# A selective-scan layer on one Trainium2 core: the convolution's taps and part of the sums over states change engine

## The reference

```python
x, z = split(layernorm(h) @ in_proj_w)            # 2048 channels each
xc = conv_b
for k in range(4):                                # depthwise causal convolution
    xc = xc + conv_w[:, k:k+1] * xp[:, :, k:k+Lq]
xc = silu(xc)
ssm_p = xc @ x_proj_w.T                           # 64 + 16 + 16 columns, each part rms-normalised
dt = softplus(dt_r @ dt_proj_w.T + dt_bias); A = -exp(A_log)
h_t = exp(dt*A) * h_{t-1} + dt * B_t * xc_t       # 16 states for each channel, t = 0..4095
ys = sum over the 16 states of h_t * C_t
y = (ys + D_param * xc) * silu(z)
x = x + y @ out_proj_w.T
x = x + layernorm(x) @ W_dequantised.T + bias
```

## Time and profile before

| | |
|---|---|
| median of 3 runs | 4657.14 us (4652.04 to 4660.07) |
| the profiled execution | 4652.27 us, span 4650.4 us |
| TensorE matmul, share of the span | 95% |
| TensorE weight load | 86% |
| VectorE | 90% |
| ScalarE | 76% |
| GpSimd | 87% |
| granted TensorE clock, mean | 0.98 |
| DMA, queue of SP, share of 16 engines | 39.6% |

### The profile page before, as it was taken

One profiled execution on the slowest core, in us unless ns is written; L12 is line 12 of the kernel. 1 busy time (PEld: TensorE's weight loads), 2 busy tenths in 40 slices (PEclk: granted clock), 3 DMA queues, 4 the chain that ended last, 5 costly groups with the idle time before them and its releaser, 6 DMA issues.

```text
span 4650.4 us, 80289 instructions
## 1 busy us (share of the span) xinstructions
PE 4425.4 (95%) x26656; PEld 4020.1 (86%) x26656; DVE 4164.3 (90%) x5745; ACT 3537.7 (76%) x8848; POOL 4034.5 (87%) x2942
## 2 busy tenths in 40 slices
PE   7788999999999999999999999999999999998879
PEld 6577889989898998989899898998989899897769
DVE  3899999999999999999999899999999999999871
ACT  3787787877878787787878878787887878777650
POOL 0898989989899998989899899999989999899870
PEclk9889999999999999999999999999999999999889
DMA  7324344353544435353444535335353443533232
GB/s 252 135 82 160 104 156 147 121 184 129 184 137 159 147 129 179 137 181 128 150 156 137 186 122 184 128 131 191 120 184 129 175 144 115 184 129 135 96 106 84
DMA packets 160286, 678.57 MB, mean 146 GB/s; under 512 B 21120, under 2 KB 30080, under 8 KB 110720
## 3 DMA queue, kind: packets, MB, share of 16 engines
q1 hardware_dynamic: 141440, 639.88, 39.6%
q10 hardware_dynamic: 18432, 33.56, 1.9%
HBM read 618.32 MB, written 55.05 MB: 145 GB/s over the span
## 4 chain that ended last, share of the span: by engine, by line
PE 65%; DVE 14%; POOL 8%; issue 7%; DMA 3%; ACT 2%; SPq 1%; POOLq 0%; DVEq 0%; ACTq 0%
PE gx L594 15%; PE ys L574 13%; PE g L767 12%; PE ys L614 12%; DVE hb L1378 9%; PE g L689 6%; POOL dbx L486 5%; DVE hc L1326 3%; POOL half L494 2%; PE ys L604 2%; PE ys L624 2%; PE hb L875 1%; DVE gx L1270 1%; DMA b_scratch<-ssmT 1%; DMA ybuf<-in_wf_scales 1%
## 5 line engine op out<-in xcount | busy, mean ns | idle before, releaser
L1378 DVE TENSOR_TENSOR_SCAN hb<-hb,dbx 128x512 f32<-128x512 f32 x2048 | 2496.7, 1219 | 110.8 <-ACT hb L1083 77.2
L486 POOL TENSOR_TENSOR dbx<-dtx,bb 128x1024 f32<-128x1024 f32 x1024 | 2421.2, 2364 | 68.9 <-DVE hb L1378 43.9
L1083 ACT ACTIVATE hb<-dt,a_neg 128x256 f32<-128x256 f32 x4096 | 1789.3, 468 | 66.3
L494 POOL TENSOR_TENSOR half<-hc 128x512 f32<-128x512 f32 x1024 | 1305.3, 1275 | 86.0 <-DVE hc L1326 85.1
L1326 DVE TENSOR_TENSOR hc<-hb,cb 128x512 f32<-128x512 f32 x2048 | 1376.2, 672 | 0.0
L574 PE MATMUL ys<-half,ident 128*128 128x256 f32 x4096 | 1057.2, 390 | 115.4 <-POOL half L494 99.1
L574 PEld LDWEIGHTS ys<-half,ident 128*128 128x128 f32 x4096 | 764.1, 194 | 242.9 <-POOL half L494 131.4
L767 PEld LDWEIGHTS g<-wo,ybuf 128*128 128x128 f32 x7680 | 909.3, 194 | 27.5 <-issue 15.2
L614 PE MATMUL ys<-xnT,wz 128*128 128x256 f32 x4096 | 931.5, 381 | 1.3 <-DVE ybuf L1337 1.3
L594 PE MATMUL gx<-xnT,wx 128*128 128x256 f32 x3968 | 903.6, 382 | 21.8 <-issue 11.0
L767 PE MATMUL g<-wo,ybuf 128*128 128x128 f32 x7680 | 915.0, 277 | 9.0 <-issue 9.0
(11 more groups left out here) (105 smaller groups left out, 2739.1 us busy)
## 6 DMA issues: line engine op xcount, KB each, us to landing
wz<-in_win SPq DMA_DIRECT2D x128, 1024.0 KB, 4.8
wx<-in_win SPq DMA_DIRECT2D x124, 1024.0 KB, 4.8
wo<-in_wout SPq DMA_DIRECT2D x123, 1024.0 KB, 5.0
wf<-wf_scratch SPq DMA_DIRECT2D x113, 512.0 KB, 3.9
xc_scratch<-xcn ACTq DMA_DIRECT2D x128, 256.0 KB, 3.7
xcs<-xc_scratch SPq DMA_DIRECT2D x128, 256.0 KB, 5.0
bb<-bc_scratch SPq DMA_DIRECT2D x64, 512.0 KB, 8.8
cb<-bc_scratch SPq DMA_DIRECT2D x64, 512.0 KB, 8.0
```

What stands on the lines that cost most here:

```text
L486: nc.gpsimd.tensor_tensor(dbx[:, k % 2, :].rearrange("p (n t) -> p n t", n=NQ), dtx[:, S % 2, a, :].unsqueeze(1).to_broadcast([P, NQ, T]), ...
L494: nc.gpsimd.tensor_tensor(half[:, k % 4, :], hc[:, k % 2, 0:HALF], hc[:, k % 2, HALF:GW], ALU.add).then_inc(halves, 1)
L1083: ins = nc.scalar.activation(h[:, m * T:(m + 1) * T], dt[:, j % 2, a, :], ACT.Exp, scale=a_neg[:, ds((2 * j + a) * N + 2 * v + m, 1)])
L1378: nc.vector.tensor_tensor_scan(h[:], h[:], dbx[:, k % 2, w * UW:(w + 1) * UW], 0.0, ALU.mult, ALU.add).then_inc(scans, 1)
```

## The change

The three taps that VectorE added become six matmuls a pair: the stationary operand is a 128x128 matrix with the tap's weights on its diagonal, the moving operand `xpre` shifted by the tap, and the result is accumulated in the pair's bank. This holds for the pairs from q = 9 on (119 of them); the first nine stay on VectorE. The diagonal matrices are made once by GpSimd from the identity, stored to DRAM and loaded again for each pair (384 KB). In return, TensorE takes only the first piece of the halves of groups 2, 3, 6 and 7, and VectorE adds the other piece (`last_sums`: two additions for each tile, the second behind the first). The gate product comes one scan later than before, and waits for these sums. In a normal step `pair_taps` stands on TensorE between `out_proj(2)` and `out_proj(3)`; in the first steps of chunks with an ffn and the last steps of chunks with a first layernorm it stands after group 4. GpSimd waits for the gate product of the tile before it overwrites a half that VectorE reads. The diff, cut to what is spoken of:

```diff
+        wt_dram = nc.dram_tensor("wt_scratch", (PAIRS, P, 2 * (KC - 1) * P), F32, kind="Internal").ap()
+        wt = sb("wt", [P, 2, KC - 1, P])
 ...
+            def store_taps(b):
+                sp.wait_ge(wt_made, after(b + 1))
+                sp.wait_ge(wt_st, landed(b))
+                sp.dma_start(wt_dram[b], made_weights(b)).then_inc(wt_st, 16)
+
+            def load_taps(q):
+                if q > PAIRS + 1:
+                    sp.wait_ge(taps_mm, after(q - PAIRS - 1))
+                sp.dma_start(wt[:].rearrange("p a k b -> p (a k b)"), wt_dram[q % PAIRS]).then_inc(wt_in, 16)
 ...
             store_scaled(PAIRS - 1)
+            store_taps(PAIRS - 1)
+            sp.wait_ge(wt_st, landed(PAIRS))
+            load_taps(PAIRS + 1)
             sp.wait_ge(z_mm, after(1))
 ...
+                    if nx.x_job(nx_last):
+                        load_taps(S + PAIRS + 2)
                     if nx.next_scan(nx_last):
                         sp.wait_ge(z_mm, after(S + 2))
 ...
+            for b in range(PAIRS):                       # GpSimd, at the start
+                if b >= 5:
+                    pool.wait_ge(wt_st, landed(b - 4))
+                nc.gpsimd.tensor_tensor(
+                    made_weights(b).rearrange("p (a k b) -> p a k b", a=2, k=KC - 1),
+                    ident[:].unsqueeze(1).unsqueeze(1).to_broadcast([P, 2, KC - 1, P]),
+                    convw[:, 2 * b * KC:2 * (b + 1) * KC].rearrange("p (a k) -> p a k", a=2)[:, :, 0:KC - 1]
+                    .unsqueeze(3).to_broadcast([P, 2, KC - 1, P]), ALU.mult).then_inc(wt_made, 1)
 ...
             def group_sum(S, k):                         # GpSimd
                 pool.wait_ge(hcs, after(UNITS * S + 2 * k + 2))
                 pool.wait_ge(sum_mm, after(8 * S + k - 3))
+                if k % NQ >= NQ - 2:
+                    pool.wait_ge(y_ready, after(2 * S + k // NQ))
 ...
                 pe.wait_ge(halves, after(8 * SG + k + 1))
-                for i in range(2):
+                for i in range(1 if q >= NQ - 2 else 2):
 ...
+            def pair_taps(q):                            # TensorE
+                pe.wait_ge(tap0, after(q + 1))
+                pe.wait_ge(wt_in, landed(q - PAIRS))
+                for a in range(2):
+                    for tap in range(KC - 1):
+                        mm = nc.tensor.matmul(gx[:, a * T:(a + 1) * T], wt[:, a, tap, :], xpre[:, a, tap:tap + T],
+                                              start=False, stop=(tap == KC - 2), skip_group_check=True)
+                mm.then_inc(taps_mm, 1)
 ...
                         group(3)
                         dt_proj()
                         out_proj(2)
+                        x_taps()
                         out_proj(3)
                     z_in_proj(1)
                     group(4)
+                    if edge:
+                        x_taps()
                     z_in_proj(0)
                     group(5)
 ...
+            def last_sums(SP, a):                        # VectorE
+                n = 2 * (2 * SP + a)
+                for i in range(2):
+                    k = NQ * a + NQ - 2 + i
+                    dve.wait_ge(sum_mm, after(8 * SP + NQ * (a + 1)))
+                    dve.wait_ge(halves, after(8 * SP + k + 1))
+                    dve.wait_ge(summed, after(n + i))
+                    nc.vector.tensor_tensor(ys[a][:, 0:T], ys[a][:, 0:T], half[:, k % 4, T:HALF], ALU.add
+                                            ).then_inc(summed, 1)
 ...
                     scan(2)
                     product(1)
+                    late_sum()
+                    scan(3)
                     late_y()
-                    scan(3)
                     product(2)
 ...
                     product(9)
                     if not (last and st.norm1):
+                        last_sums(S, 0)
+                    scan(11)
+                    if not (last and st.norm1):
                         y_gate(S, 0)
-                    scan(11)
                     product(10)
                     scan(12)
+                    if last and st.norm1:
+                        last_sums(S, 0)
                     product(11)
                     if last and st.norm1:
                         y_gate(S, 0)
-                    if not edge:
-                        taps()
```

More of the change, by code:

```diff
@@ L236, in build_program, with made_weights @@
         dequant = ybuf[:, 4:6, :].rearrange("p a t -> p (a t)")
+        def made_weights(b):
+            place = 6 + 2 * (b % 5)
+            return ybuf[:, place:place + 2, :].rearrange("p a t -> p (a t)")[:, 0:2 * (KC - 1) * P]
         flat = [t[:].rearrange("p a b -> p (a b)") for t in (wf, wx, wz, bb, cb, wo)]
@@ L456, in _ @@
                                     pattern=[[-1, P]], channel_multiplier=1).then_inc(id_ready, 1)
+            pool.wait_ge(id_ready, after(1))
+            pool.wait_ge(consts_in, landed(8))
+            for b in range(PAIRS):
[6 more added lines that the diff above has]
+                    .unsqueeze(3).to_broadcast([P, 2, KC - 1, P]), ALU.mult).then_inc(wt_made, 1)
             def first_inflows(S):
@@ L594, in pair_in_proj @@
                     mm = nc.tensor.matmul(pair_bank(q)[:, a * T:(a + 1) * T], pair_weights(q)[:, kk, a * P:(a + 1) * P],
-                                          xnT[:, chunk % 2, kk, :], start=(kk == 0), stop=(kk == KH - 1))
+                                          xnT[:, chunk % 2, kk, :], start=(kk == 0 and a == 0), stop=(kk == KH - 1),
+                                          skip_group_check=True)
                 if a == 1:
                     mm.then_inc(x_mm, 1)
+            def pair_taps(q):
[6 more added lines that the diff above has]
+                mm.then_inc(taps_mm, 1)
             def pair_proj(q):
@@ L786, in ss_transpose, with x_taps @@
                             chunk_ss(c + 1)
+                    def x_taps():
+                        if st.x_job(last):
+                            pair_taps(S + PAIRS + 1)
+                    edge = last and st.norm1 or first and st.ffn
                     ffn()
@@ L949, in norm_evac, with wait_taps @@
                                bank[:].rearrange("p (k t) -> p k t", k=4)).then_inc(evac, 1)
+            def wait_taps(n):
+                if n <= PAIRS + 1:
+                    act.wait_ge(conv, after(6 * n))
+                else:
+                    act.wait_ge(taps_mm, after(n - PAIRS - 1))
             def pair_taps(q):
@@ L969, in pair_silu @@
             def pair_silu(q):
-                act.wait_ge(conv, after(6 * (q + 1)))
+                wait_taps(q + 1)
                 act.wait_ge(xp_mm, after(q))
@@ L1388, in late_product, with late_sum @@
                             times_c(S - 1, UNITS - 1)
+                    def late_sum():
+                        if was.scan and not (first and c == 0):
+                            last_sums(S - 1, 1)
                     def late_y():
@@ L1392, in late_y @@
                             y_gate(S - 1, 1)
-                    def taps():
-                        if st.x_job(last):
-                            pair_conv(SX)
                     def add_ffn():
@@ L1435, in norm_stats @@
                             norm2_aggregate(c - 1)
-                    edge = first and st.ffn or last and st.norm1
                     scan(0)
@@ L1481, in step @@
                     product(13)
-                    if edge:
-                        taps()
                     scan(15)
```

18 lines of the change are left out of this document (12 added, 6 removed).

## The result

The changed kernel takes 4992.41 us (median of 4 runs, 4991.17 to 4993.65); the kernel before takes 4655.44 us beside it. The ratio is 1.072, with a 95% interval of 1.0705 to 1.0742. The profiled execution has a span of 4991.0 us, 340.6 above the 4650.4 of before. The forecast was 4912, which is +255 against +337 measured. The result lies above the 4860 to 4985 that the forecast gave for its own case, and 8 us inside the outer range of 4750 to 5000.

The account below looks back on a forecast made before the run. TensorE was taken as the bound, with VectorE tied to it by its wait for the ffn. Normal steps 190, edges 44 and 23, start +5, early chunks -10, end +3 gave +255: 4912 us, range 4860 to 4985, outer 4750 to 5000.

Parts of the forecast that it names:

- its own case: Group 3's sum on TensorE waits for GpSimd's half 3, delayed by VectorE's additions: 4912 us, chance 0.72.
- The bound of before: TensorE has no idle time in a normal step of 33.20 us; VectorE waits 1.00 us for the ffn.
- faster: Rival: VectorE is the real bound and TensorE has room, so the gain is 88 us: 4570 us, chance 0.04.
- The normal step: 78 steps, j = 1 to 6 of chunks 2 to 14: period 35.64 us, +2.44 each, 190 us in all.
- `x_proj`'s wait: In normal steps TensorE's `x_proj` waits for the later gate product; covered by group 3's wait, no cost.
- VectorE's wait at `add_ffn`: Sign in a normal step: VectorE's wait for the ffn grows from 1.0 to about 4.2 us.
- The edges: Chunks' last steps +3.66 us each (12, 44 in all), first steps about +1.8 each (13, 23 in all).
- Chunks 0 and 1: VectorE sets chunk 0 and nearly chunk 1; its work falls by 0.74 us a step: -10 us.
- Start and end: Start: SP waits for the last tap weights, +5 us; chunk 14's last step and chunk 15: +3 us.
- Only the work counts: Rival: TensorE stays without idle time and only its added work costs, +88 and +5 us: 4750, chance 0.12.
- The change's own waits cancel: Rival: TensorE's extra work fits in the edges; time within 0.2%, 4657 us, chance 0.02.
- The clock: Rival: TensorE's new waits in normal steps bring half pace behind them, about +130 more: 5040 us, chance 0.10.

## Why the prediction was right, and where it was off

**The bound of before** was right. One matmul off TensorE and off the path gives exactly its 0.43 us a step, and taps alone cost exactly their 2.59. This answers the rival *faster* too. By the Trainium skill (Trainium Kernel Development and Optimization, Best Practices) a kernel's distance from the roofline is to be judged by its MFU (the share of peak arithmetic) and the busy share of weight loads; the latter stood at 90% here, yet there was no tenth of TensorE to be had. The pace from start to start was the better view.

**The normal step** came out as worked out, 35.64 us against 35.64. That it agrees to the hundredth is in part luck: the pair takes 0.90 us, not 0.80, half 3 follows product 7 sooner by 0.08 us and is 0.02 shorter, and the three cancel. The idle time of TensorE is 1.5 us, of which 0.4 stands before `x_proj` (3.95 us from `out_proj` to `x_proj`, 3.57 usual) and 1.0 before group 3, where the forecast had 1.4 in one place. That `x_proj`'s wait adds nothing of its own held, since both waits lie in the same cycle. The taps don't wait for `tap0`. VectorE's wait at `add_ffn` grew to 2.93 us in the step shown (3.07 in others), not 4.2: ScalarE holds a scan up later in the step. From 1000 to 3900 us the waits by engine, line and releaser (us in total, times, longest) show both:

```profile
DVE x L1374 <- PE g L744: 261.8, 77, 6.7
DVE hb L1461 <- ACT hb L1153: 122.1, 107, 3.7
PE ys L615 <- POOL half L534: 49.0, 59, 0.9
```

**The edges** are the term that was mis-sized. The forecast was right on when the gate product comes: `x_proj` starts 8.38 us after the ffn in the last step, 6.37 before, +2.01 against +1.93. What it missed is the pace behind the wait. It had half pace as a rival for the normal steps alone, and put the matmuls behind the edges' waits at full pace, though by its own terms these waits are longer than the normal steps' 1.4 us (in the last step 0.47 + 1.93, and the 0.86 saved ahead of it: 3.26, measured 3.35). Against the kernel before, the last step has `x_proj` +0.86, half of `out_proj` +1.65, the transposes +0.21, together 2.72; 2.01 + 2.59 - 0.86 + 2.72 = 6.46, and the step grew by 43.34 - 36.89 = 6.45 (forecast 3.66). The first step: `out_proj` +1.54; with the forecast's 1.8 that is 3.3, and it grew by 43.00 - 39.32 = 3.68. Over chunks 2 to 13 that is 12 x (2.72 + 1.54) = 51 of the 60 us missing there.

**Chunks 0 and 1** were forecast at -10 and came out at +8.5. The forecast counted VectorE's work and left out that the late additions stand in a cycle there too: GpSimd's half 7, TensorE's group 7, the additions, and from product 8 by way of ScalarE to GpSimd's next operand. With the taps alone both chunks get shorter (-2.2 and -6.5), with the sums alone longer (+11.3 and +7.1), and with the taps and the early pair shorter again (-0.8 and -8.3). That the late pair, with the gate product behind it, causes it is shown; the way round the cycle is read from the trace and was not tested.

**Start and end** were near (+6.5 and +5.3, against +5 and +3).

**The rivals.** *Only the work counts* (4750) fell: versions with 110 and 221 us more work on TensorE were faster. *The change's own waits cancel* (4657) fell with the 337 us. *The clock* (5040) did not hold in the normal steps, where waits of 0.4 and 1.0 us are followed by full pace, but half pace came at the edges, which took 43.3 and 43.0 us where 40.6 and 41.1 were forecast, and the version with the gate product ahead of scan 3 shows how near the normal steps are to it. The Trainium skill (TensorE: Matmul & The Clock Gate, Part 1) makes the half clock the default and activity what lifts it. This case's granted clocks of 0.50 and 0.72 behind idle time and 1.00 in unbroken stretches agree, but full pace also came behind long waits, one of them 3.35 us (last section).

## What to carry to other kernels

Before work is moved off the busiest engine, find the path that ties the engines together once a period, and ask on which side of it the work lands: the same addition gained 0.43 us a step behind product 9 and nothing behind product 1. Two halves of a trade are priced apart: here the taps cost 2.59 us a step and the sums that were to pay for them gave back 0.15 us a normal step and took 7 us a chunk at the edges. And where a wait on TensorE grows to a few microseconds, price the matmuls behind it at half pace too, as a case of its own.

## What the runs showed of the hardware

- A wait's length alone doesn't decide the pace behind it. Over all kernels here, from 1000 to 3900 us, the granted clock in the first microsecond behind a wait of TensorE was under 0.9 in 4 of 1313 waits of 0.15 to 1.4 us, in 18 of 91 of 1.4 to 2, in 19 of 29 of 2 to 3.1, and in 82 of 83 longer ones. (A fall that comes later, as after the 1.49 us above, isn't counted.) The one exception is this `x_proj`, in the version with the unused addition off the path, where the same wait elsewhere is followed by half pace:

```profile
2761.98 1.13 PE L660 MATMUL ys<-xprojw,xcn 128*128 128x96 f32 x8 [3.35 <-DVE ybuf L1422]
```

- With the last step back at full pace (`out_proj(0)` ahead of `x_proj`), `out_proj` one step later went from about 5.2 us to between 6.2 and 6.3 in eleven of thirteen chunks, behind an unchanged wait of 3.83 in most of them. That the one caused the other isn't shown: with the unused addition off the path, where `x_proj` keeps its wait, the same `out_proj` takes between 5.1 and 6.4.
- A VectorE addition of 128x512 with both operands in SBUF takes 1.08 us beside GpSimd's half sum and 1.45 within GpSimd's work (medians of 1.09 and 1.45; single ones 0.68 to 1.94), where the product of the same size with an operand in PSUM takes 0.67. The one addition with no GpSimd instruction beside it took 0.68. The Trainium skill (GPSIMD Engine Reference, Specifications) says that the two engines share their SBUF interfaces and contend when a VectorE instruction has two SBUF inputs; the two durations agree.
- Two dependent VectorE additions of 128x256 in PSUM take 0.98 us, 0.90 to the next start, where two at the pace of the gate's row would take 0.66.
